# Attention scores from stacked fp16 halves, with 1,024-wide maxima and exponentials

## What is computed

```python
x = x + jnp.tanh(g_xattn[0]) * _L0_xattn_ref(_layernorm(x, axis=-1), ctx_512, ctx_512)
x = x + jnp.tanh(g_ffn[0]) * _L0_ffn_ref(_layernorm(x, axis=-1), ...)
# _L0_xattn_ref
scores = jnp.einsum('bkgsd,bktd->bkgst', qh, kh) / scale
weights = jax.nn.softmax(scores, axis=-1)
out = jnp.einsum('bkgst,bktd->bkgsd', weights, vh)
```

## Time and profile before

| | |
|---|---|
| median of 3 runs | 1436.35 us (1429.1 to 1441.07) |
| the profiled execution | 1441.87 us, of which the span is 1440.1 us |
| mean granted clock of TensorE in it | 0.941 of full speed |
| attention, first product to last | 8 to 454 us |
| router stage | 454 to 509 us |
| experts | 509 us to the end |
| PE busy | 1353.0 us (94%) |
| DVE busy | 878.3 us (61%) |
| ACT busy | 519.9 us (36%) |
| POOL busy | 465.0 us (32%) |

### The profile page before, as it was taken

The page is one execution under the profiler, slowest core; times in us unless marked ns, Lnnn a source line. Parts: engine busy times, 40 slices in busy tenths (PEclk is TensorE's granted clock), DMA queues, the critical chain, the costliest instruction groups (busy, mean ns, idle before and its releaser), DMA issues.

```text
span 1440.1 us, 33203 instructions
## 1 busy us (share of the span) xinstructions
PE 1353.0 (94%) x11762; PEld 989.7 (69%) x11762; DVE 878.3 (61%) x1737; ACT 519.9 (36%) x949; POOL 465.0 (32%) x373
## 2 busy tenths in 40 slices
PE   4789999999996889989999999999999999999996
PEld 3456666666652767777777777777777777777773
DVE  3767767777755886854545555544444444446887
ACT  2256656676653522222222222222222222222220
POOL 2147777777773700011111111111111111004454
PEclk9979989999985579999999999999999999999998
DMA  7224434444342741136255363546163631167666
GB/s 244 94 90 139 144 116 140 141 158 135 132 144 78 260 164 60 59 134 204 81 181 183 131 204 102 198 145 219 58 211 124 200 106 58 44 211 235 212 206 189
DMA packets 98782, 213.59 MB, mean 148 GB/s; under 512 B 10800, under 2 KB 12336, under 8 KB 98736
## 3 DMA queue, kind: packets, MB, share of 16 engines
q1 hardware_dynamic: 87536, 176.28, 36.0%
q0 software_dynamic: 11200, 36.71, 8.2%
HBM read 228.26 MB, written 66.06 MB: 204 GB/s over the span
## 4 chain that ended last, share of the span: by engine, by line
PE 89%; DVE 5%; issue 2%; DMA 2%; ACT 1%; POOL 1%; SPq 0%; DVEq 0%; ACTq 0%; POOLq 0%
PE PS L1351 38%; PE PS L1370 19%; PE PS L1193 8%; PE PS L1205 8%; PE PS L1215 5%; PE PS L1339 3%; PE PS L1226 3%; PE PS L1175 2%; DVE st L752 1%; DMA xnd<-xhl 1%; PE PS L1236 1%; PE PS L1296 1%; DVE negm L807 1%; POOL xhl L545 1%; PE PS L1164 1%
## 5 line engine op out<-in xcount | busy, mean ns | idle before, releaser
L1370 PE MATMUL PS<-wb,ghl 128*128 128x512 f16 x1296 | 293.1, 383 | 7.5 <-DVE ghl L1055 4.3
L1351 PE MATMUL PS<-xT,wb 128*128 128x256 f16 x2592 | 293.8, 274 | 1.1 <-DVE xT L1033 1.1
L1351 PE MATMUL PS<-uhl,wb 128*128 128x256 f16 x2592 | 291.8, 273 | 1.0 <-DVE uhl L1043 1.0
L1351 PEld LDWEIGHTS PS<-xT,wb 128*128 128x128 f16 x2592 | 254.5, 98 | 31.8 <-issue 1.3
L1351 PEld LDWEIGHTS PS<-uhl,wb 128*128 128x128 f16 x2592 | 251.4, 98 | 29.6 <-DVE uhl L1043 1.3
L807 DVE TENSOR_REDUCE negm<-PS 128x4 f32<-128x512 f32 x256 | 164.9, 686 | 117.5 <-PE PS L1193 114.9
L1370 PEld LDWEIGHTS PS<-wb,ghl 128*128 128x128 f16 x1296 | 127.8, 99 | 152.8 <-issue 14.1
L560 POOL COPY ixr<-idx 128x2 int32 x38 | 7.0, 184 | 606.9 <-PE PS L1339 478.2
L1205 PE MATMUL PS<-qT,kT 17*128 17x512 f32 x512 | 182.7, 690 | 16.5 <-ACT Pt L625 13.5
L625 ACT ACTIVATE Pt<-PS 128x512 f32<-128x512 f32 x256 | 140.1, 607 | 156.7 <-PE PS L1205 156.2
L1193 PE MATMUL PS<-kT,qT 16*128 16x128 f32 x2048 | 162.8, 300 | 8.0 <-DVE negm L807 8.0
(11 more groups left out here) (142 smaller groups left out, 1397.2 us busy)
## 6 DMA issues: line engine op xcount, KB each, us to landing
wb<-wsc SPq DMA_DIRECT2D x126, 1024.0 KB
wst<-in_wall SPq DMA_DIRECT2D x32, 768.0 KB, 5.6
wsc<-whl SPq DMA_DIRECT2D x32, 768.0 KB, 4.2
ysl<-yb SPq DMA_DIRECT2D x46, 512.0 KB
bd<-in_bdown SPq DMA_DIRECT2D x42, 256.0 KB
X<-in_x SPq DMA_DIRECT2D x8, 1024.0 KB, 8.8
xnd<-xhl SPq DMA_DIRECT2D x32, 256.0 KB, 2.9
xs<-xnd SPq DMA_DIRECT2D x32, 256.0 KB
```

The lines of the kernel that those rows point to most:

```text
L1351: ins = pe.matmul(bank[:, hf, (m % 2) * TT:(m % 2 + 1) * TT], wb[:, par, l, k, w, m * P:(m + 1) * P], rhs(x, k), start=(n == 0), stop=(n = ...
L1370: ins = pe.matmul(PS[2][:, t, :], ghl[:, x, k, t * P:(t + 1) * P], wb[:, par, 2, k, w, :], start=(n == 0), stop=(n == len(TERMS) - 1))
```

## The change

The scores are no longer fp32 products. The normalised queries and the keys are split into an fp16 value and an fp16 remainder. A strip of the transposed queries holds 16 rows of values and 16 of remainders (`qT`), and there are two arrays of keys (`kT`): the value twice, and the remainder. A score is then two fp16 passes, one of 32 rows and one of 16. The negated maxima are a third pass of one row, a tile `negR` multiplied by ones.

The maxima and the exponentials are one instruction of 1,024 elements per unit where they were two of 512. With that, one semaphore step stands for a whole unit: products into `Mb` wait until the last unit's reduction has ended, products into `Tb` until its exponential has. `scores` writes the passes of a unit's transposed scores with the products for the next unit's maxima in between: two passes' products, then six for the maxima, three times.

The splitting is new work: ACT writes the values (`high`), DVE a normalised fp32 copy of the queries (`norm1`), POOL the remainders (`split_kq`). `tr_k` and `tr_q` transpose fp16. The evacuation of all queries is one ACT instruction of 1,024 elements (`evac_q`), where DVE took half. `weights64` moves from POOL to DVE. `high` stands behind the body's first exponential; `queries` stood ahead of it. In the diff `...` marks what is left out.

```diff
+            def split_kq(half, par):
...
+                need(g, S["tk_done"], b - 1)
+                g.wait_ge(S["kh_ready"], b + 1)
...
+                g.tensor_tensor(kx[:, par, 1, :, 0, :], cv, kx[:, par, 0, :, 0, :], ALU.subtract).then_inc(S["k_split"], 1)
+                g.wait_ge(S["qh_ready"], b + 1)
+                g.wait_ge(S["xn_ready"], b + 1)
...
+                g.tensor_tensor(qx[:, par, :, :, 1, :].rearrange("p m k d -> p k m d"), xv,
+                                qx[:, par, :, :, 0, :].rearrange("p m k d -> p k m d"), ALU.subtract).then_inc(S["q_split"], 1)
...
                 if after is not None:
                     values(*after)
+                    split_kq(*after[:2])
                 if not start:
                     weights_lo(*pv)
-                weights64(half, par)
-                if not start:
                     residual(*pv)
...
+            def high(half, par):
...
+                act.activation(kx[:, par, 0, :, :, :], cv.unsqueeze(2).to_broadcast([P, NKV, 2, D]), ACT.Copy).then_inc(S["kh_ready"], 1)
...
+                act.wait_ge(S["t_done"], n + 1)
+                act.activation(Pt[:, u, :, :].rearrange("p h s -> p (h s)"), Tb[:, :, :].rearrange("p o c -> p (o c)"), ACT.Exp,
+                               scale=float(D) ** -0.5).then_inc(S["exp_done"], 1)
...
+                exps(half, par, 0)
                 if after is not None:
-                    queries(*after[:2])
-                exps(half, par, 0)
+                    high(*after[:2])
...
+            def norm1(half, par):
...
+                v.tensor_scalar(xn32[:, par, :], X[:, bass.ds(b, 1), :].rearrange("p o c -> p (o c)"), ln[:, 0, bass.ds(b, 1)],
+                                ln[:, 1, bass.ds(b, 1)], ALU.mult, ALU.add).then_inc(S["xn_ready"], 1)
...
+                v.wait_ge(S["m_done"], UNITS * b + u + 1)
+                v.tensor_reduce(negm[:, u // 2, u % 2 * 8:u % 2 * 8 + 8], Mb[:, :, :].rearrange("p o (m t) -> p (o m) t", t=CTX),
+                                AX.X, ALU.max, negate=True).then_inc(S["max_done"], 1)
...
+            def weights64(half, par):
+                v.wait_ge(w_in[par], 16 * (half + 1))
+                v.tensor_scalar(wst[:, par, :, :], wst[:, par, :, :], WS, None, ALU.mult).then_inc(S["w64_ready"], 1)
...
+            def tr_k(half, par):
+                b = 2 * half + par
+                pe.wait_ge(S["k_split"], b + 1)
...
+            def scores(half, par, quad, u, ahead):
...
+                if ahead is not None:
+                    max_waits(*ahead[:2], ahead[3])
+                pe.wait_ge(neg_in[u // 2], 16 * (b + 1))
+                need(pe, S["exp_done"], UNITS * b + u)
+                for p in range(3):
                     for odd in range(2):
...
+                    if ahead is not None:
+                        for n in ((0, 1, 2), (3, 4, 5), (6, 7))[p]:
+                            ins = max_head(ahead[2], ahead[3], n // 2, n % 2)
...
-                scores_T(half, par, quad, 0)
-                if nx is not None:
-                    scores_max(*nx, 1)
+                scores(half, par, quad, 0, nx and (*nx, 1))
                 if not start:
                     tr_o(*pv[:2], 0)
                 if after is not None:
-                    tr_k(*after)
+                    tr_k(*after[:2])
+                scores(half, par, quad, 1, nx and (*nx, 2))
                 if not start:
                     outputs(*pv, 1)
-                scores_T(half, par, quad, 1)
+                if after is not None:
+                    tr_q(*after[:2])
```

More of the change, by code:

```diff
@@ L640, in weights_hi @@
                 act.activation(whl[:, par, :, 0, :], wst[:, par, :, :], ACT.Copy).then_inc(S["whi_ready"], 1)
[L642 to L645, removed]
+            act.wait_ge(S["vone"], 4)
+            act.wait_ge(c_in[0], 16)
+            high(0, 0)
+            high(0, 1)
+            evac_q(0, 0, 0)
+            evac_q(0, 1, 1)
             act.wait_ge(S["wrs_ready"], 1)
@@ L661, in body @@
                 if after is not None:
-                    evac_q0(*after)
+                    evac_q(*after)
                 exps(half, par, 2)
@@ L852, in body @@
                 start = isinstance(half, int) and number(half, par) == 0
+                if after is not None:
+                    norm1(*after[:2])
                 if nx is not None:
@@ L862, in body @@
                     maxes(*nx[:2], 2)
-                    evac_neg(*nx[:2], 0)
-                if not (isinstance(half, int) and number(half, par) < 2):
-                    stats2(half - 1, par)
+                weights64(half, par)
                 if nx is not None:
                     maxes(*nx[:2], 3)
+                    evac_neg(*nx[:2], 0)
                 if not start:
@@ L871, in body @@
                     maxes(*after[:2], 0)
+                if not (isinstance(half, int) and number(half, par) < 2):
+                    stats2(half - 1, par)
                 if nx is not None:
                     evac_neg(*nx[:2], 1)
-                if after is not None:
-                    evac_q1(*after)
             over_batches(v, body)
@@ L1181, in strip, with max_head, max_waits @@
                 return slice(STRIP * s, STRIP * s + rows)
-            def scores_max(half, par, quad, u):
+            def max_head(quad, u, m, w):
+                rows = (STRIP, D)[w]
+                for odd in range(2):
+                    part = strip(u, odd, rows)
+                    ins = pe.matmul(Mb[:, odd, m * P:(m + 1) * P], qT[part, quad, u // 2, m, :], kT[part, quad, w, u // 2, :],
+                                    start=w == 0, stop=w == 1)
+                return ins
+            def max_waits(half, par, u):
@@ L1198, in scores_T @@
-            def scores_T(half, par, quad, u):
-                b = number(half, par)
-                pe.wait_ge(neg_in[u // 2], 16 * (b + 1))
-                for odd in range(2):
-                    need(pe, S["exp_done"], 2 * (UNITS * b + u) + odd - 1)
-                    rows = strip(u, odd, D + 1)
-                    pe.matmul(Tb[:, odd, :], kT[rows, quad, u // 2, :], qT[rows, quad, u // 2, :, :].rearrange("p m c -> p (m c)"),
-                              start=True, stop=True).then_inc(S["t_done"], 1)
+                    max_head(quad, u, m, 0)
```

193 lines of the change are left out of this document (92 added, 101 removed).

## The result

The changed kernel takes 1483.1 us (median of 4 runs, 1482.3 to 1484.5). The kernel before took 1433.0 us beside it (median of 4, 1429.1 to 1441.1). The ratio is 1.033 with a 95% interval of 1.030 to 1.037. The change makes the kernel slower.

What follows compares the result with a forecast made beforehand. PE was taken as the bound. Batches of 14.7 us (two thirds of the time) and 11.9 (one third) average 13.6 against 11.79: +53, -2 and +1 make +52; 1441.9 + 52 - 5.5 = 1488 us, 8 in 10 from 1432 to 1530.

Steps and rivals of the forecast that it cites:

- mean batch: Attention: two thirds of the time at 14.7 us a batch and one third at 11.9 make 13.6, against 11.79 before.
- share of the lower level: Attention: PE's clock at the lower level two thirds of the time, between none and all; called the largest uncertainty.
- new wait for the keys: At the lower clock PE can't begin unit 1 until `tr_k` is through at 4.0 us, though `tr_o` ended at 2.6.
- The other term of the sum: Full-clock batches, one third of the time: 11.9 us each, with DVE held at `weights64` and unit 3 waiting for its reduction.
- forecast sign of `weights64` at 2 us or more: On DVE wherever the clock is full: `weights64` lasts 2 us or more, ending 0.8 us behind POOL's `weights_lo`.
- That it would alternate: Attention: PE's clock switches between levels, as PE works 7.5 of 11.9 us at the full clock, 13.6 of 14.7 at the lower.
- a PE that works all the time (clock back): Kernel before: PE busy all the time got the full clock back; busy three quarters of 85 us, it stayed at 0.50.
- The hold of `weights64`: DVE's multiplication waits for a POOL instruction it meets, on a shared port pair: POOL's end plus 0.84 us, 1.1 alone.
- saved on POOL is worth nothing, since POOL had slack: Full-clock batch: taking `weights64` (4.09 us) off POOL gains nothing, because POOL had slack.
- Pieces that don't overlap: Rival: maxima products queue between score passes; a unit costs 2.4 us at the lower clock, kernel over 1600 us; chance 0.06.
- The clock holds: Rival: clock stays as it was, DVE is held; a batch takes 11.9 or 12.4 us, kernel 1437 to 1453; chance 0.17.
- DVE not held: Rival: `weights64` slips in ahead of POOL's subtraction; full-clock batch 10.1 us, 10.5 at today's mean clock, kernel 1397; chance 0.15.

Runs made afterwards that it cites:

- e2: The changed kernel with ACT's rounding of keys and queries ahead of the body's first exponential: 1396.4 us, ratio 0.972.
- e3: The changed kernel with twenty needless fp16 products of 128 columns a batch, placed where PE waits: 1446.3 us, ratio 1.009.
- e1: The changed kernel with the multiplication of the weights by 64 moved back from DVE to POOL: 1493.1 us, ratio 1.042.
- e5: The changed kernel with both the rounding ahead of the first exponential and twenty needless products a batch: 1374.8 us, ratio 0.958.
- e8: The changed kernel with the rounding first, and maxima and exponentials in halves with a semaphore step each: 1461.7 us, ratio 1.020.
- e7: The changed kernel with all 16 products for the maxima written behind the three passes instead of between them: 1483.5 us, ratio 1.036.
- e11: e2 with POOL's subtraction of the weights in three instructions instead of one: 1418.3 us, ratio 0.980.
- e10: e5 with the needless products doubled from 20 to 40 a batch: 1376.0 us, ratio 0.958.

## Why the prediction was right, point by point

| step | predicted | measured |
|---|---|---|
| kernel | 1488 us | 1483.1 us |
| mean batch | 13.6 us | 13.64 us |
| unit of scores, lower and full level | 1.5, 0.83 | 1.40 (261.20 to 262.60), 0.75 (268.13 to 268.88) |
| outputs, lower level | 1.87 | 1.86 (262.60 to 264.46) |
| wide exponential, reduction | 1.02, 1.2 | 1.02, 1.23 |
| first unit to second, lower level | 4.0 | 4.16 (257.04 to 261.20) |
| `weights64` alone | 1.1 | 0.94 to 0.95 |
| `weights64` held | POOL's end + 0.84 | POOL's end + 0.82 |
| share of the lower level | 2/3 | 0.74 (clock 0.63) |
| full-level batch, `weights64` held | 11.9 us | none ran |

**The batch** at the lower level came out as forecast in place and size. The new wait for the keys stands behind the first exponential; by the forecast's own times it was 0.9 us at the lower level and 1.4 at the full one, and the rows have 1.12 and 1.49. The long batches, 14.4 to 14.6 us, are almost wholly at the lower level (14.7 was worked out). The score piece was a little too dear, and the share of the lower level, which the text called a choice, a tenth too small; these pull in opposite directions.

The other term of the sum, a third of the time at 11.9 us a batch, was not borne out. The full level came in stretches of not quite 7 us around the last unit and the first, none of the 24 `weights64` fell into one, and so none held up unit 3, which is what made the forecast's 11.9. Such a stretch made its batch 12.8 us instead of 14.5, 1.7 us less; at the forecast's two rates it would have given 1.6. The agreement of the two is luck, and that the sum lands within 5 us of the median is partly this luck. The forecast sign of `weights64` at 2 us or more was not seen in this kernel.

**The clock.** That it would alternate is what the rows show: lost behind a stretch with PE busy for 63%, back behind one with 93%. That gaps in PE's work cost clock is borne out by two interventions: taking the wait away (e2) and filling it with needless products (e3) both raised it, and both shortened the kernel. That less work means less clock is not: in e1 PE was busy for less and the clock was higher. The reasoning was weaker than the outcome. It set a PE that works all the time (clock back) against one that works three quarters of it (clock stays). By windows of these runs, busy for 86% went with 1.00 for 250 us (e5), 85% with 0.63 (the changed kernel), 74% with 0.73 (e1), and 97% with 0.50 for 80 us (e8). The busy share of a long window doesn't order the clock, not least because the same work is busy for longer at the lower level. What does was not found.

**The hold of `weights64`** has the mechanism and the price as written, in 1.85 us rows of this kernel and 2.6 us ones of e3. What it costs depends on the level: nothing in this kernel, as the forecast said of the lower clock, and DVE's time in e3. The Trainium skill's rule (SBUF — State Buffer, section on the two separate sides) holds here: the trace agrees, in the 0.82 us behind POOL's end and in the 0.73 us by which POOL's parts lengthen in turn. One sentence on it was wrong: what it "saved on POOL is worth nothing, since POOL had slack". With the splitting on POOL that slack is gone, and leaving the multiplication there costs some 10 us more (e1). The slack was read from the kernel before and not worked out for the one after.

**The rivals.** Pieces that don't overlap: fell, 0.75 and 1.40 us a unit, and e7 shows it even without the interleaving. The clock holds: fell for this kernel. e3 comes near it by hand, and its 1446.3 us lies in the 1437 to 1453 that was worked out; but its clock was 0.82 and it has twenty products more, so this is in part luck. DVE not held: fell. A full-clock batch of 10 us did appear, but by putting the values first.

**What the forecast left unused.** It named the order of `high` behind the exponential as the cause of the new wait and did not work out what another order would bring. That was 87 us, more than the slowdown itself: some 38 us for the wait, and the rest with the clock.

## What to carry to other kernels

When a product gets cheaper, work out what PE waits for in its place: taking away a wait of 1.3 us a batch gave more than twice its own length, as the clock went with it. Where PE must wait, needless products in the gap can pay (37 us here, 22 us with the shorter wait), and doubling them cost nothing. The slack of an engine has to be worked out for the kernel after the change, since other moves of the same change may have filled it. And a long instruction costs only where something waits behind it: look at the idle time after it before counting it.

## What the runs showed of the hardware that was not expected

- By the records, PE started products for two free strips 0.02 us after the first pass of two other strips, although four more passes were written ahead of them; what they released came in the order written (e7). Interleaving by hand brought nothing.
- PE busy for 97% of 80 us kept a clock of 0.50 (e8), while in the earlier trace rows PE busy the whole time had it back, and PE busy for 86% of 250 us had 1.00 throughout (e5). What the difference rests on was not found.
- Some kernels scatter with the clock: e11 ran from 1395.3 us at a mean clock of 0.939 to 1429.4 at 0.883, e2 from 1386.3 at 0.948 to 1409.8 at 0.909. Others do not: the changed kernel, whose levels alternate regularly, spread over 2.2 us, and the one with doubled products (e10), at the full level throughout, over the same.
